# Linear attention step on one core: output tiles ahead of the query product, additions to x early, phi last

## The reference

```python
q = hidden_states @ Wq.T + bq
k = hidden_states @ Wk.T + bk
v = hidden_states @ Wv.T + bv
k = _repeat_kv(k, b, s); v = _repeat_kv(v, b, s)
sq = elu_plus_one(q)                      # phi of the query
sk = elu_plus_one(k)
kv = jnp.einsum('bhsd,bhse->bhde', sk, v)
qkv = jnp.einsum('bhsd,bhde->bhse', sq, kv)
k_sum = sk.sum(axis=2)
norm = jnp.einsum('bhsd,bhd->bhs', sq, k_sum)
attn = qkv / (norm[..., None] + EPS)
attn = attn.transpose(0, 2, 1, 3).reshape(b, s, H * D)
return attn @ Wo.T
```

## Time and profile before

| | |
|---|---|
| median of 3 runs | 3533.94 us (3533.3 to 3534.62) |
| the profiled execution | 3533.81 us, span 3532.1 us |
| TensorE granted clock, mean | 0.979 of full speed |
| linear attention, first query product to last output tiles | 94.47 to 713.18 us |
| busy in the whole span | TensorE 95%, VectorE 75%, ScalarE 58%, GpSimd 30% |

### The profile page before, as it was taken

One profiled execution on the slowest core, in us unless ns is written; L12 is line 12 of the kernel. 1 busy time (PEld: TensorE's weight loads), 2 busy tenths in 40 slices (PEclk: granted clock), 3 DMA queues, 4 the chain that ended last, 5 costly groups with the idle time before them and its releaser, 6 DMA issues.

```text
span 3532.1 us, 52701 instructions
## 1 busy us (share of the span) xinstructions
PE 3343.3 (95%) x19398; PEld 2864.0 (81%) x19398; DVE 2663.9 (75%) x4951; ACT 2045.8 (58%) x3907; POOL 1054.9 (30%) x1268
## 2 busy tenths in 40 slices
PE   3898999989999999999999999999999999999993
PEld 3777878868888888888888888888888888888882
DVE  5788796767876787876778677886788767876764
ACT  3676767646556565556555656556555565556551
POOL 4786656631122122122121212212111221122103
PEclk8999999999999999999999999999999999999995
DMA  2221112110000000000000110000000000000001
GB/s 82 71 83 57 58 57 70 54 37 13 13 22 28 13 16 13 14 25 25 13 13 13 31 42 16 14 14 28 22 14 13 23 26 26 13 25 23 26 7 30
DMA packets 98525, 104.21 MB, mean 30 GB/s; under 512 B 10336, under 2 KB 88800, under 8 KB 98144
## 3 DMA queue, kind: packets, MB, share of 16 engines
q1 hardware_dynamic: 98272, 100.85, 9.6%
HBM read 87.18 MB, written 13.63 MB: 29 GB/s over the span
## 4 chain that ended last, share of the span: by engine, by line
PE 70%; DVE 5%; ACT 3%; issue 1%; POOL 0%; DMA 0%; DVEq 0%; SPq 0%; POOLq 0%; ACTq 0%
PE at_ps_job L1752 12%; PE at_ps_job L35 7%; PE at_ps_job L37 7%; PE at_ps_job L36 7%; PE at_ps_o L35 6%; PE at_ps_o L37 6%; PE at_ps_o L36 6%; PE at_ps_s L35 6%; PE at_ps_s L36 6%; PE at_ps_s L37 6%; DVE at_neg_max L1684 1%; ACT x_resident L1618 1%; DVE at_probT_lo L1629 1%; PE at_ps_job L645 1%; DVE at_oT_lo L1660 0%
## 5 line engine op out<-in xcount | busy, mean ns | idle before, releaser
L1575 ACT ACTIVATE at_probT_hi<-at_ps_job 128x512 fp32r<-128x512 f32 x1024 | 611.4, 598 | 890.2 <-PE at_ps_job L1752 887.8
L1629 DVE TENSOR_TENSOR at_probT_lo<-at_ps_job,at_probT_hi 128x512 fp32r<-128x512 f32 x1024 | 702.7, 686 | 275.6 <-ACT at_probT_hi L1575 265.1
L1618 ACT ACTIVATE x_resident<-at_ps_s,at_neg_max 128x1024 f32<-128x1024 f32 x512 | 570.7, 1115 | 151.1 <-DVE at_neg_max L1684 145.9
L1684 DVE TENSOR_REDUCE at_neg_max<-at_ps_s 128x1 f32<-128x1024 f32 x512 | 622.1, 1215 | 5.3
L1752 PE MATMUL at_ps_job<-ident,x_resident 128*128 128x128 f32 x4096 | 613.8, 272 | 5.0 <-DVE at_probT_lo L1629 3.2
L1752 PEld LDWEIGHTS at_ps_job<-ident,x_resident 128*128 128x128 f32 x4096 | 495.9, 140 | 97.7 <-issue 7.3
L35 PE MATMUL at_ps_o<-at_probT_hi,at_v_lo 128*128 128x512 f32 x1024 | 446.3, 436 | 8.9 <-DVE at_oT_lo L1660 7.8
L1558 POOL TENSOR_TENSOR at_w_hi<-at_w_raw,ch_cols 128x256 fp32r<-128x256 f32 x192 | 117.6, 613 | 1120.5 <-PE at_ps_job L37 1099.8
L35 PE MATMUL at_ps_s<-at_k_hi,at_q_lo 128*128 128x512 f32 x1024 | 445.1, 435 | 0.0
L37 PE MATMUL at_ps_o<-at_probT_lo,at_v_hi 128*128 128x512 f32 x1024 | 404.7, 395 | 0.0
L36 PE MATMUL at_ps_s<-at_k_hi,at_q_hi 128*128 128x512 f32 x1024 | 402.0, 393 | 0.0
(11 more groups left out here) (274 smaller groups left out, 7485.9 us busy)
## 6 DMA issues: line engine op xcount, KB each, us to landing
at_w_raw<-attn_w SPq DMA_DIRECT2D x256, 128.0 KB, 2.3
at_w_raw<-mlp_w SPq DMA_DIRECT2D x112, 128.0 KB, 2.3
li_wo_hi<-li_wo_kept SPq DMA_DIRECT2D x24, 256.0 KB, 2.7
li_wo_lo<-li_wo_kept SPq DMA_DIRECT2D x24, 256.0 KB, 3.0
li_wq_hi<-li_wq_kept SPq DMA_DIRECT2D x48, 128.0 KB, 2.2
li_wq_lo<-li_wq_kept SPq DMA_DIRECT2D x48, 128.0 KB, 2.8
x_resident<-x SPq DMA_DIRECT2D x4, 1024.0 KB, 13.1
out<-x_resident SPq DMA_DIRECT2D x4, 1024.0 KB, 4.9
```

The lines of the kernel that those rows point to most:

```text
L1575: nc.scalar.activation(ph[:, i // TC, 4 * half:4 * half + 4, (i % TC) * P:(i % TC + 1) * P], c.turned_bank(2 * TB * u + 2 * i + half), ACT ...
L1618: nc.scalar.activation(prob[:, slot % 2, :], ps_s[slot % 2][:], ACT.Exp, bias=nmax[:, slot:slot + 1], accum_out=rsum[:, u % 2, slot:slot + ...
L1629: nc.vector.tensor_tensor(pl[at], c.turned_bank(2 * TB * u + 2 * i + half), ph[at].bitcast(F32), ALU.subtract).then_inc(s_pl, 1)
L1684: nc.vector.tensor_reduce(nmax[:, slot:slot + 1], ps_s[slot % 2][:], AX.X, ALU.max, negate=True).then_inc(s_max, 1)
```

## The change

In each step TensorE makes the four output tiles of m = t - 2 before the query product, and `step_claims` numbers them in that order. ScalarE takes the denominators ahead of the relu and the exponential, and the fourth tile (`ybuf`) right behind them. VectorE takes the reciprocals and the three additions right behind the evictions; phi of the query is its last instruction of the step. `rnorm` gets two halves, used in turn, with waits on the additions two steps back in place of those one step back.

```diff
 def step_claims(t):
-    if 0 <= t < LOOP * B:
-        yield ("QUERY", t), "phi", t + 1
     m = t - LAG
     if 0 <= m < LOOP * B:
         for j in range(3):
             yield ("OUT", m, j), "x", 3 * m + j + 1
         yield ("OUT", m, 3), "y3", m + 1
+    if 0 <= t < LOOP * B:
+        yield ("QUERY", t), "phi", t + 1
...
-        rnorm = sb("rnorm", [P, TC], F32)
+        rnorm = sb("rnorm", [P, 2, TC], F32)
...  ScalarE
                 evict(t)
                 act_evict(nc, act, c, t)
+                if y_step(t):
+                    act.wait_ge(s_y, t - LAG + 1)
+                    if t > LAG:
+                        act.wait_ge(s_rn, t - LAG)
+                    for own, banks in out_banks(t - LAG):
+                        last = nc.scalar.activation(norm[:, own], ps[:, banks, D], ACT.Copy, bias=ATT_EPS)
+                    last.then_inc(s_norm, 1)
                 if q_step(t):
...
                 if y_step(t):
-                    act.wait_ge(s_y, t - LAG + 1)
-                    if t > LAG:
-                        act.wait_ge(s_rn, t - LAG)
-                    for own, banks in out_banks(t - LAG):
-                        last = nc.scalar.activation(norm[:, own], ps[:, banks, D], ACT.Copy, bias=ATT_EPS)
-                    last.then_inc(s_norm, 1)
+                    m = t - LAG
+                    act.wait_ge(s_rn, m + 1)
+                    if m >= 2:
+                        act.wait_ge(s_x3, m - 1)
+                    nc.scalar.activation(ybuf[:, m % 2, :], c.own_bank(("OUT", m, 3))[:, 0:D], ACT.Copy,
+                                         scale=rnorm[:, m % 2, 3:4]).then_inc(s_y3, 1)
                 if t - 1 in kv_time:
...
                 act_background(nc, act, c, t)
-                if y_step(t):
-                    m = t - LAG
-                    act.wait_ge(s_rn, m + 1)
-                    if m >= 2:
-                        act.wait_ge(s_x3, m - 1)
-                    nc.scalar.activation(ybuf[:, m % 2, :], c.own_bank(("OUT", m, 3))[:, 0:D], ACT.Copy, scale=rnorm[:, 3:4]).then_inc(s_y3, 1)
...  VectorE
                 evict(t)
                 dve_evict(nc, dve, sh, c, t)
+                if y_step(t):
+                    m = t - LAG
+                    dve.wait_ge(s_norm, m + 1)
+                    if m >= 2:
+                        dve.wait_ge(s_y3, m - 1)
+                        dve.wait_ge(s_x, 3 * m - 3)
+                    nc.vector.reciprocal(rnorm[:, m % 2, :], norm[:]).then_inc(s_rn, 1)
+                    dve.wait_ge(s_rn, m + 1)
+                    for j in range(3):
+                        x = x_tile_of(m, j)
+                        nc.vector.scalar_tensor_tensor(x, c.own_bank(("OUT", m, j))[:, 0:D], rnorm[:, m % 2, j:j + 1],
+                                                       x, ALU.mult, ALU.add).then_inc(s_x, 1)
                 if t - 2 in kv_time:
...
-                if y_step(t):
-                    (the same, with one rnorm, and with waits for s_y3 >= m and s_x >= 3 * m)
...  TensorE
             for t in range(BEGIN, plan.end):
+                if y_step(t):
+                    (the four output tiles, as before)
                 if q_step(t):
...
-                if y_step(t):
-                    (the four output tiles)
                 for kind, v, part in rows.get(t, []):
```

More of the change, by code:

```diff
@@ L1319, in _ @@
             for t in range(BEGIN, plan.end):
+                if y_step(t):
+                    m = t - LAG
+                    head = m // 2 % H
+                    pe.wait_ge(s_pl, m + 1)
+                    if m % 4 == 0:
+                        pe.wait_ge(c.taken, by_dve["MADE", m // LOOP * KVH + head // GQ, head // 2 % 2])
+                    for j in range(TC):
+                        wait_emptied(pe, c, plan.claim["OUT", m, j])
+                        ts = slice(j * P, (j + 1) * P)
+                        last = split3(nc, c.own_bank(("OUT", m, j))[:, 0:MW], ph[:, m % (LAG + 1), ts], pl[:, m % (LAG + 1), ts],
+                                      mh[:, head, :], ml[:, head, :], start=True, stop=True)
+                    last.then_inc(s_y, 1)
                 if q_step(t):
```

## The result

The changed kernel takes 3579.62 us (median of four runs, 3578.26 to 3582.32) against 3533.62 us (3532.89 to 3534.62) for the kernel before on the same chip: a ratio of 1.0131, interval 1.0113 to 1.0148. It is 46.0 us slower. The forecast of 3547 us had the direction (+13.6 us) and not the size; 3579.62 lies beyond the range's 3572. The profiled execution took 3579.92 us, its span is 3578.2.

A forecast was written before the change was run, and what follows sets the result against it. The prediction saw a loop over VectorE and ScalarE that TensorE bumps into. Its terms, 9.6 + 6 + 8 + 4 - 14 = +13.6 us on about 3534, gave 3547 us, range 3512 to 3572.

The forecast's parts named there:

- (a): PSUM banks: TensorE's waits for the bank that f empties mostly go, 32.1 us at best, nothing at worst.
- (b): VectorE's order: a new gap behind f, about 0.8 us before the reciprocal, 1.2 where an eviction needs ScalarE first.
- (c): Steps 64 to 87, worked through on 64 to 67: 0.4 us a step slower, +9.6 us over 24 steps.
- (d): Layer norms (L97) lose 27 us to GpSimd; about half comes back, with the sum 13 us lower or higher at the ends.
- (e): Steps 24 to 31 and 40 to 47: no key/value product fills the gap, 16 steps at 0.4, +6 us.
- (f): Steps 112 to 127, short: output tiles need phi one query product earlier, a two-step loop; together +8 us.
- (g): Single pairs of short steps elsewhere (45/46, 61/62, 77/78, 109/110): the same two-step loop, eight steps at 0.5, +4 us.
- (h): Outside saturated stretches, TensorE waiting less for banks gives back 14 us of the 32 idle, between 0 and 30.
- list of signs: What would show the forecast right, including TensorE's waits for phi_lo above 20 us and for f's bank under 10.
- its own ends: The forecast's own range for the whole kernel, 3531 to 3563 us, by the ends of (d) and (h).
- Of the rivals, 3: Slower still: VectorE's gap hides nowhere in the 128 steps, 98 us of gaps, phase +28, 3562 us; chance 0.13.
- Rival 1: Faster: decoupling wins through the banks in the linear-attention loop, -26 us, 3508 us; chance 0.28.

The follow-up runs named there:

- denominators first: The changed kernel with ScalarE taking the denominators ahead of phi_hi of the step before, at the head of its step: 3585.93 us, ratio 1.0148.
- lag 3: The changed kernel with output tiles using a phi one step older (LAG = 3 instead of 2) and shared loading buffers: 3560.37 us, ratio 1.0076.
- cover of the evictions: The changed kernel with denominators first, and VectorE's reciprocal and three additions put ahead of the evictions: 3573.18 us; 3538.7 us with lag 3.

## Where the prediction was right and where it failed

By its own steps, with f-to-f distances for the stretches:

- **(a)** As said: TensorE's wait for f's bank fell from 32.1 to 8.0 us, under the 10 foretold. No run shows that this was worth time by itself.
- **(b)** Right in mechanism and in the size of one gap: 0.76 to 0.82 us ahead of the reciprocal in the last steps and 1.18 us ahead of an xnT_lo. The reciprocal's waits are 63.2 us in all (59.9 in the 128 steps), within the 40 to 90 named. The evictions' part is nearly as large: the low parts' waits rose from some 26 us to 74.5 (69.8 shown above, and 4.7 for xnT_lo).
- **(c)** Steps 64 to 87: +8.0 us measured, +9.6 foretold. The run with the denominators first took 5.9 of it back, so the cause is in the main the one named.
- **(d)** The 64 layer norms took 38.1 us instead of 49.9:

```profile
L97 DVE TENSOR_SCALAR ch_r<-x_resident,ln_mean,ln_rstd 128x256 f32<-128x256 f32 x40 | 20.1, 552 | 0.0
L97 DVE TENSOR_SCALAR li_xn<-x_resident,ln_mean,ln_rstd 128x256 f32<-128x256 f32 x24 | 18.0, 790 | 0.0
```

  11.8 us came back, a little under the half of 27 that was counted on. This term spoke for the change, and in size it held; 11.8 us of work less still did not make the phase shorter, since VectorE idled 62 us more.
- **(e)** Steps 24 to 31 and 40 to 47: +7.3 us against +6. The sum is right and the cause only in part. Nearly all of it (+5.5) lies in 24 to 31, and there lag 3 alone gives 5.4 back: it was in the main phi_lo, not the gap behind f. The sum came out by luck.
- **(f)** Steps 112 to 127: +7.0 us against +8, 63.94 us by the windows where 65 and more was said. Lag 3 takes 2.5 back, so the two-step loop through phi_lo is a part of it.
- **(g) and (h)** The step that failed is (h), the -14 us for banks. It fell to the other four stretches together, with half of (g)'s +4 (its steps 45, 46, 77 and 78 lie in stretches already named), so they were put at -12; measured is 9.4 + 3.2 + 4.6 + 7.3 = +24.5 us. That is 36.5 us of miss, more than the 32 us by which the whole sum is short. (h) asked what TensorE gains when it need not wait for banks, and answered 14 of 32 us. It didn't ask what then stands at the head of TensorE's step. (f) had named it, the output tiles that need phi one query product sooner, and (f) and (g) priced it for short steps only, as a loop; the list of signs even has waits for phi_lo above 20 us. But a wait for phi_lo comes just as well where one heavy step on VectorE or GpSimd makes a single phi late, as the 3.49 us in steps 24 to 26 show, and uneven stretches are where (h) booked a gain. In the 128 steps TensorE saved 24.1 us on f's bank and waited 59.9 - 4.0 = 55.9 more for phi_lo. Lag 3 takes 10.2 of the 24.5 us back. The second part of the miss is that the gaps of (b) have no term of their own in these stretches. The cover of the evictions takes some 5 us back there (denominators first, lag 2), nearly all of it in steps 0 to 23 (139.2 to 133.8 us). The remaining 9 us stay open, as far as terms from two different orders can be added.

One more thing in the sum: its own ends, 3531 to 3563 us, are narrower than (d) and (h) make them. With (h) at nothing and every norm beside GpSimd it would be 3547 + 14 + 13 = 3574 us, and the measured time lies beyond even that.

Of the rivals, 3 was the nearest (3562 us). It put VectorE's gaps at 98 us; the reciprocal's and the low parts' waits together rose by 63 + 48 = 111 us, while the wait for the exponential, which it counted with the rest, fell from 60.7 to 18.5. So it had the right engine, but neither it nor any other case had TensorE's wait for phi_lo in its price. Rival 1 is refuted as a whole, and yet a part of what spoke for it was true: with only ybuf or the reciprocal moved, so that ScalarE no longer makes phi_hi wait behind ybuf, the kernel before gains 15 to 19 us. (Both runs also have two halves of rnorm. VectorE did not wait ahead of the reciprocal in the 128 steps before, so the trace gives them nothing to bring; they were not run alone.)

## What to carry to other kernels

In a loop over several in-order queues, moving an instruction early for the sake of its consumer puts it in front of others: ask of the new head of each queue what it waits for in the worst step, not in the mean one. A transfer of slack (a bank wait against an operand wait) is no gain until the second is priced over the same stretches as the first. And where one small result gates another engine, move that one alone: a reciprocal of 0.17 us ahead of an instruction of 0.75 us brought 0.55%, while the reordering around it lost 1.3%.

## What the runs showed of the hardware

TensorE's granted clock fell after such a wait. The windows of the changed kernel around the 3.49 us of idle time ahead of 237.88:

```profile
232.00:236.00 4.00, 2.39 (x15) 1.77 (x13) 3.21 (x11) 1.59 (x5) 3.74 (x5) 1.00 0.12 40
...
238.00:242.00 4.00, 4.00 (x16) 3.71 (x17) 1.60 (x5) 1.50 (x4) 4.00 (x5) 0.50 0.01 2
...
244.00:248.00 4.00, 4.00 (x30) 3.73 (x29) 3.21 (x8) 3.41 (x8) 2.04 (x3) 1.00 0.20 68
```

At 0.50 (1.2 GHz) TensorE issued 16 matmuls in 4 us, at 1.00 (2.4 GHz) 30. The shapes are mixed differently in the two; for one and the same shape, start to start, a 258-column matmul took 0.21 us (238.26 to 238.47) and later 0.12, a 512-column one 0.43 (240.62 to 241.05) and later 0.23. This makes steps 24 to 31 worse than the wait alone (mean clock 0.88, before 0.95). Over all 128 steps the mean is 0.97 in both, but that is rounded: length times what the clock is short of full speed, added up over the ten stretches of each kernel, gives about 17 us before and 23 after, an estimate that the rounding makes good to some 3 us on either side. The lower clock could thus be a part of the 6 us left open above; no run separates it.

The shared ports reach further than the layer norm that the prediction counted. phi of keys (L1275, both tensors in SBUF) takes 0.42 us at 104.96 and 1.20 us at 116.44. GpSimd had ended its last instruction at 104.61 and was idle beside the first, and ran a 128x512 subtraction beside the second:

```profile
104.96 0.42 DVE L1275 SCALAR_TENSOR_TENSOR li_z<-li_z,li_ekk 128x256 f32<-128x256 f32 x1
...
116.44 1.20 DVE L1275 SCALAR_TENSOR_TENSOR li_z<-li_z,li_ekk 128x256 f32<-128x256 f32 x1
...
116.25 1.10 POOL L1108 TENSOR_TENSOR li_kv_lo<-li_z,li_kv_hi 128x512 fp32r<-128x512 f32 x1
```

The Trainium skill, "SBUF — State Buffer", section "Who interferes with whom", says that a VectorE instruction with two SBUF inputs contends with a GpSimd instruction that reads SBUF. The traces agree in kind: the 56 instructions of this form in the phase took 726 ns on average after the change and 756 before, against the 0.42 us of the one that ran alone.
